# How far ahead GpSimd adds the bias to residual tiles: one tile or three

## The reference

```
w = weights[subjects]                       # 32 sequences, one 128x128 matrix each
y = einsum('bct,bcd->bdt', x, w)            # x: 32 x 128 x 2048, float32
result = einsum('bnd,od->bno', y, W_base) + b_base
probs = softmax(einsum('bnd,ed->bne', y, W_gate)); top 2 of 8, renormalised -> route_w
h = einsum('bnd,erd->bner', y, A); delta = einsum('bner,eor->bno', h * route_w, B)
out = x + result + delta * SCALING
```

## Time and profile before

| | |
|---|---|
| median of 3 runs | 1715.55 us |
| the profiled execution | 1715.63 us, span 1713.5 us |
| TensorE (PE) busy | 1538.2 us, 90% of the span |
| VectorE (DVE) busy | 1266.5 us, 74% |
| GpSimd (POOL) busy | 630.6 us, 37% |
| ScalarE (ACT) busy | 594.9 us, 35% |
| mean granted TensorE clock | 0.963 of full |

### The profile page before, as it was taken

One profiled execution on the slowest core, in us unless ns is written; L12 is line 12 of the kernel. 1 busy time (PEld: TensorE's weight loads), 2 busy tenths in 40 slices (PEclk: granted clock), 3 DMA queues, 4 the chain that ended last, 5 costly groups with the idle time before them and its releaser, 6 DMA issues.

```text
span 1713.5 us, 25586 instructions
## 1 busy us (share of the span) xinstructions
PE 1538.2 (90%) x9475; PEld 832.8 (49%) x9475; DVE 1266.5 (74%) x2138; ACT 594.9 (35%) x996; POOL 630.6 (37%) x531
## 2 busy tenths in 40 slices
PE   5269999999999899999955999999999999999998
PEld 4155454444444444444545555555554455555553
DVE  4566766666767676777666788888888888888875
ACT  6463323233232333333267333332233333232231
POOL 2244554544455555545445122222222222222222
PEclk9579999999999999999988999999999999999999
DMA  5142434333344443344362333334443433334432
GB/s 199 71 139 87 128 121 127 112 102 105 120 130 130 130 124 116 120 122 127 125 215 73 93 118 114 96 100 130 130 129 105 118 118 112 99 98 130 130 102 68
DMA packets 102909, 201.85 MB, mean 118 GB/s; under 512 B 10874, under 2 KB 24186, under 8 KB 102266
## 3 DMA queue, kind: packets, MB, share of 16 engines
q1 hardware_dynamic: 102786, 200.22, 38.0%
HBM read 128.96 MB, written 71.22 MB: 117 GB/s over the span
## 4 chain that ended last, share of the span: by engine, by line
PE 47%; DVE 20%; issue 19%; POOL 8%; ACT 4%; DMA 1%; POOLq 0%; SPq 0%; DVEq 0%; ACTq 0%
PE bank_x L986 6%; PE bank_x L988 6%; PE bank_x L987 6%; DVE s_parts L688 5%; PE bank_y L988 4%; PE bank_y L986 4%; PE bank_y L987 4%; POOL x_res L432 4%; POOL x_res L422 4%; DVE t_sums L711 3%; DVE t_sums L715 2%; PE bank_h L986 2%; PE bank_h L988 2%; PE bank_h L987 2%; PE bank_z L988 2%
## 5 line engine op out<-in xcount | busy, mean ns | idle before, releaser
L432 POOL TENSOR_TENSOR x_res<-x_res,t_sums 128x512 f32<-128x512 f32 x256 | 354.5, 1385 | 604.3 <-DVE t_sums L715 347.2
L986 PE MATMUL bank_x<-TT,s_parts 128*128 128x512 f16 x768 | 298.8, 389 | 63.7 <-ACT p_copies L512 50.4
L987 PE MATMUL bank_x<-TT,s_parts 128*128 128x512 f16 x768 | 298.1, 388 | 0.0
L988 PE MATMUL bank_x<-TT,s_parts 128*128 128x512 f16 x768 | 297.7, 388 | 0.0
L986 PE MATMUL bank_y<-TT,s_parts 128*128 128x512 f16 x768 | 291.1, 379 | 0.2 <-ACT p_copies L512 0.2
L987 PE MATMUL bank_y<-TT,s_parts 128*128 128x512 f16 x768 | 291.1, 379 | 0.0
L988 PE MATMUL bank_y<-TT,s_parts 128*128 128x512 f16 x768 | 291.1, 379 | 0.0
L497 ACT ACTIVATE s_parts<-a_full 128x512 f16<-128x512 f32 x224 | 140.9, 630 | 336.6 <-DVE a_full L693 185.7
L512 ACT ACTIVATE p_copies<-bank_x,y_inv 128x512 f32<-128x512 f32 x128 | 87.5, 684 | 434.6 <-PE bank_x L988 344.9
L422 POOL TENSOR_TENSOR x_res<-x_res,BT 128x512 f32<-128x512 f32 x128 | 184.4, 1441 | 118.2 <-issue 116.2
L715 DVE TENSOR_TENSOR t_sums<-t_sums,inv_w 128x512 f32<-128x512 f32 x256 | 219.3, 857 | 8.8
(11 more groups left out here) (209 smaller groups left out, 2663.1 us busy)
## 6 DMA issues: line engine op xcount, KB each, us to landing
x<-in_x_dram SPq DMA_DIRECT2D x32, 1024.0 KB, 5.9
x_res<-in_x_dram SPq DMA_DIRECT2D x128, 256.0 KB, 3.7
part_scratch<-x_res SPq DMA_DIRECT2D x128, 256.0 KB, 3.6
x_res<-part_scratch SPq DMA_DIRECT2D x128, 256.0 KB, 4.0
out_dram<-x_res SPq DMA_DIRECT2D x128, 256.0 KB, 2.9
x_res<-in_L_ffn_W_base_dram SPq DMA_DIRECT2D x12, 512.0 KB, 4.6
w_cond<-in_L_cond_weights_dram SPq DMA_DIRECT2D x64, 64.0 KB, 4.0
a_full<-in_L_ffn_W_base_dram SPq DMA_DIRECT2D x8, 512.0 KB, 4.9
```

The costliest lines, as they stand in the source:

```text
L432: nc.gpsimd.tensor_tensor(XR[:, xr_slot(m), :], XR[:, xr_slot(m), :], TM[:, m % 2, :], ALU.add).then_inc(r_added, 1)
L986: nc.tensor.matmul(dst, lhs[0], rhs[0], start=start, stop=False, skip_group_check=chained)
L987: nc.tensor.matmul(dst, lhs[0], rhs[1], start=False, stop=False, skip_group_check=chained)
L988: return nc.tensor.matmul(dst, lhs[1], rhs[0], start=False, stop=stop, skip_group_check=chained)
```

## The change

GpSimd adds the bias three tiles ahead of the product it is about to add, and carries on across the boundary of steps. The number of adds stays the same.

```diff
+AHEAD = 3
...
                 if n < NP:
-                    add_bias(8 * n)
                     for j in range(8):
-                        if j < 7:
-                            add_bias(8 * n + j + 1)
+                        if n == j == 0:
+                            for early in range(AHEAD):
+                                add_bias(early)
+                        if 8 * n + j + AHEAD < 8 * NP:
+                            add_bias(8 * n + j + AHEAD)
                         add_r(8 * n + j)
```

## The result

The change makes the kernel **slower**: 1724.79 us, the median of 5 runs (1724.25 to 1727.11), against 1715.6 us, the median of 5 runs of the kernel before; the ratio is 1.0054 (95% interval 1.0039 to 1.0069), some 9 us. The number lies inside my range, but on the side that I had given 0.28. The profiled execution has a span of 1722.1 us, 8.6 us more than before.

What follows compares the result with a forecast made beforehand. It took a loop through GpSimd to bound pass 1 at 46.18 us a step, and a slot loop of 45.46 to replace it: 1715.63 - 10.8 + 2.7 = 1707.5, rounded to 1707 us, range 1688 to 1732.

Steps and rivals of the forecast that it cites:

- The floor of 42.1 us a step: Pass 1: the step TensorE alone would allow, 46.18 us less a 3.15 us stop and 0.9 us of slow clock.
- the loop through GpSimd: Pass 1, 46.18 us a step: sharing, adds, VectorE, ScalarE, TensorE's last product, finishes of t6 and t7, maxima, sharing again.
- One add less behind the sharing: Ahead of t0's product add, one bias instead of two: both VectorE waits 1.33 us shorter, 20 us over 15 steps.
- The second loop: Pass 1: loads, stores and adds through GpSimd, SP and six slots bind at 45.46 us a step, 10.8 us won.
- rival B: Loads come in time often enough: loop 44.0 us if t9's load lands in 3.1 us, total 1685 us; chance 0.12.
- to end of r2 (t5's load): From t0's to t2's product add: load issue 3.81 us, landing 4.1, then t5's bias and t2's product add; 10.56 us.
- to end of r4 (t7's load): From t2's to t4's product add: issues 0.45 us, landing 3.6, t7's bias 1.3, t4's product add 1.6; 7.0 us.
- to end of r6 (t9's load): From t4's to t6's product add: issue 0.4 us, landing 4.6, t9's bias 1.7, t6's product add 1.6; 8.35 us.
- rival C: Pass 1: slots bind harder through t5's late load, deciding from a 46.0 us loop; at 46.96, 1730 us; chance 0.28.
- the likeliest case: Pass 1: the slots' loop takes over just under the old one; 1707 us, 1698 to 1712; chance 0.42.
- The first step: Start of pass 1: four biases instead of two ahead of the first product add, 2.7 us more, once.
- I count nothing: End of pass 1: the last three product adds have no bias ahead, weren't late before, so no gain was counted.

Runs made afterwards that it cites:

- a table of biases: Against the kernel before: a table sets how many bias adds stand ahead of each product add, none ahead of a step's first; 1669.29 us, ratio 0.9735.
- one ahead, through: Against the kernel before: bias adds stay one tile ahead but carry on across the steps, so one moves from behind the sharing; 1695.95 us, ratio 0.989.

## Why the prediction was wrong

*What bounded the kernel: right.* The floor of 42.1 us a step and the loop through GpSimd stand; a table of biases brought the step to 42.8.

*One add less behind the sharing: right in its worth.* r0 starts 15.6 us after the sharing's start, as forecast, and alone the move is worth 19 of the 20 us. That both of VectorE's waits get shorter by 1.33 us was wrong: with one ahead, through, the wait for t2's buffer falls from 4.2 to 2.9 us in the mean, and that for t3's stays at 1.26. The sum had counted the gain once, so it wasn't hurt. And the 17.4 us that r0 took before was one long step; the mean is 16.8.

*The second loop: right in kind, mis-sized in one term.* Below are the means of the 14 steps with the change, beside the forecast. (For rival B I had written that t9's load showed 4.4 to 5.1 us in 16 steps; pass 1 has 15 such loads, with 4.5 to 5.1.)

| term | forecast | measured |
|---|---|---|
| end of r7 to end of r0 | 16.95 | 16.9 |
| to end of r2 (t5's load) | 10.56 | 10.7 |
| **to end of r4 (t7's load)** | **7.0** | **8.4** |
| to end of r6 (t9's load) | 8.35 | 8.0 |
| to end of r7 | 2.6 | 2.6 |
| step | 45.46 | 46.6 |

The term that failed is the one from r2 to r4, with 3.6 us for the landing of t7's load. t7's load landed in 5.1 us in this step (issued at 394.08):

```profile
x_res<-in_x_dram SPq DMA_DIRECT2D x1, 256.0 KB, 5.1
```

and in 4.7 in the middle of all 16 steps. t2's store and t7's load on SP, before (where the earlier trace rows have the load alone):

```profile
479.07 0.33 SPq L324 DMA_DIRECT2D part_scratch<-x_res  x1
482.41 0.33 SPq L313 DMA_DIRECT2D x_res<-in_x_dram  x1
```

And with the change:

```profile
393.71 0.33 SPq L325 DMA_DIRECT2D part_scratch<-x_res  x1
394.08 0.43 SPq L314 DMA_DIRECT2D x_res<-in_x_dram  x1
```

In the kernel before the load was issued 3.0 us behind t2's store in the mean, because SP waited for t1's store to land; with the change it leaves 0.4 us behind it, like t9's load, whose 4.7 us I had in the earlier trace rows; that was the nearer row for t7 too. The landing is 1.1 of the 1.4 us. In the sum it is this term that turns a gain of 0.75 us a step into a loss of 0.39.

*But that term alone doesn't settle it.* With t7's load issued early, r4 came 2.2 us sooner in the mean (2.8 in the step shown), and the step stayed at 46.46. The sum also lacked the path through VectorE, from r2 over t4's finish and the sums to t5. I had said of the second loop that it holds "hardly TensorE or VectorE". The stall of 5 us ahead of r2 feeds both paths, and moving that one bias behind r2 gave 20 us. The rival C, which I had given 0.28, had the mechanism (t5's load, then everything shifts) and the point of 46.0 us from which it decides. That the measured time lies inside my range is C's doing: the likeliest case had the wrong sign.

*The first step: right,* 2.5 us against 2.7. *"I count nothing" for the end of pass 1* was wrong: there is 1.3 us less to the last product add, but 2.6 us more in the second preparation. ScalarE's waits there for rows of the weight rose from 8.7 to 11.6 us, which fits SP reaching their loads late relative to the end of pass 1; I didn't test it.

*Signs.* As forecast: the 5 us wait of t5's bias, t9's of 1.2 to 3.1 us (the 1.60 us ahead of it in this step the profile puts down to VectorE), and TensorE's stop moved to `bank_c`, with 2.9 instead of 2 us. t7's bias waited 2.1 to 2.7 us instead of 1 to 2. VectorE's wait at t4's finish came (3.72 us in this step), but it didn't move there from t2 and t3: these still wait 3.0 and 1.2 us in the mean.

## What to carry to other kernels

Working further ahead in an in-order engine helps only as far as the buffers let the data be there: with six slots and a store and a load between two uses, one tile ahead across the steps won 19 us, two won 30, three lost 9 and four lost 342, 20%. When you move a step ahead of a wait, write down the loop through the buffers, take each transfer's landing from the row that leaves in the same company (right behind its store, or alone), and look for the second path that starts at the same stall. The best kernel here differs from the kernel before only in the place of GpSimd's bias adds: first the product adds that free somebody's buffer, and the bias adds behind them.

## What the runs showed of the hardware

I hadn't expected that taking away a wait for a load would make a kernel slower (1684.56 to 1692.06 us). A GpSimd that stands still is worth something to VectorE: its sums of two inputs in SBUF take 0.68 us then, and 1.75 us beside GpSimd's adds. Its operations on a PSUM bank and one input in SBUF (`t_sums<-bank_x,y_inv,p_copies`) took 0.67 to 0.75 us in pass 1 of every kernel, beside GpSimd or not.

The same 256 KB landed in 3.1 to 5.3 us in the earlier trace rows. For t7's load the landing goes with its distance from the store ahead of it: over all kernels here, 47 of these loads left 0.4 us behind t2's store and landed in 4.4 to 5.1 us, 97 left 0.7 us or more behind it and landed in 3.1 to 4.5, and the 16 that left ahead of it landed in 2.9 to 3.2. But the store alone isn't enough: t10's load follows its store as closely and landed in 3.1 us. What else lengthens t7's and t9's stays open. More slots, which would have loosened the loop directly, were not tried.
